# A two-layer cross-attention and mixture-of-experts kernel: the first experts' down product split into rounded parts, their up weights loaded tile by tile, and GpSimd's order and gathers changed

## The reference

```
x = x + attention0(layernorm(x), ctx)      # 16 heads
x = x + experts0(layernorm(x))             # top 1 of 8 by centroid; w1 (1024 x 256), relu, w2 (256 x 1024)
x = x + attention1(layernorm(x), ctx)      # 8 heads, two more layernorms, an output product
x = x + experts1(layernorm(x))             # top 2 of 8, gated by sigmoid, shared output product
```

## Time and profile before

| | us |
|---|---|
| median of 3 runs (1675.1 to 1678.51) | 1677.14 |
| the profiled execution | 1680.14 |
| its span, first to last instruction | 1678.3 |
| TensorE matmul busy (89% of the span) | 1491.0 |
| VectorE busy (60%) | 1002.0 |
| ScalarE busy (53%) | 882.1 |
| GpSimd busy (50%) | 833.9 |

### The profile page before, as it was taken

How to read it: one execution, slowest core, us unless ns; L and a number is a source line. 1 busy time by engine, 2 the same in 40 slices (tenths; PEclk the granted TensorE clock), 3 DMA queues, 4 the chain that set the end, 5 groups by cost and what they waited for, 6 DMA issues and landing times. The chain is left out here.

```text
span 1678.3 us, 50328 instructions
## 1 busy us (share of the span) xinstructions
PE 1491.0 (89%) x17142; PEld 1239.3 (74%) x17143; DVE 1002.0 (60%) x2228; ACT 882.1 (53%) x1626; POOL 833.9 (50%) x1145
## 2 busy tenths in 40 slices
PE   6999999999996499999599999999999646999677
PEld 4777777777774499999478888888888524888566
DVE  3677677677663433333247677777777577777544
ACT  3777777777774244443266566656665323333233
POOL 3576676666663111111256666666666305333263
PEclk8999999999996699999799999999999757999889
DMA  5111211110100611111212222221110042333475
GB/s 145 58 53 58 83 59 48 59 34 23 34 18 12 261 35 38 38 34 34 86 33 75 67 92 71 75 90 44 44 48 25 16 141 88 129 130 131 127 232 182
DMA packets 63184, 127.98 MB, mean 76 GB/s; under 512 B 11106, under 2 KB 35870, under 8 KB 59590
## 3 DMA queue, kind: packets, MB, share of 16 engines
q1 hardware_dynamic: 52798, 99.03, 18.2%
q0 software_dynamic: 10320, 28.07, 6.0%
HBM read 94.77 MB, written 32.29 MB: 76 GB/s over the span
## 5 line engine op out<-in xcount | busy, mean ns | idle before, releaser
L1017 DVE TENSOR_REDUCE a_mx<-a_SM 100x2 bf16<-100x722 f32 x384 | 351.4, 915 | 201.1 <-PE a_SM L459 197.8
L737 ACT ACTIVATE a_Pr<-a_ST 120x1600 f32<-120x1600 f32 (+3 forms) x192 | 225.0, 1172 | 125.5 <-PE a_ST L491 123.8
L501 PE MATMUL a_M<-a_Pr,a_V 120*32 120x100 f32 (+3 forms) x4608 | 176.2, 257 | 0.0
L459 PE MATMUL a_SM<-a_KT,a_QM 32*100 32x362 f32 x768 | 152.6, 393 | 25.9 <-DVE a_mx L1017 25.6
L787 POOL TENSOR_TENSOR a_rstd<-a_ve,a_powers 100x1 f32<-100x1 f32 x192 | 118.7, 618 | 96.2 <-DVE a_ve L986 94.5
L501 PEld LDWEIGHTS a_M<-a_Pr,a_V 120*32 120x32 f32 (+3 forms) x4608 | 135.8, 120 | 21.7 <-issue 12.8
L862 POOL TENSOR_TENSOR a_cl<-a_ct,a_ch 128x724 fp32r<-128x724 f32 x62 | 107.3, 1731 | 42.9 <-DVE a_o L1059 42.9
L386 PE MATMUL a_M<-a_wvh,a_ch 128*120 128x256 f32 (+1 forms) x384 | 123.8, 322 | 3.1 <-ACT a_KF L623 3.1
L852 POOL TENSOR_TENSOR a_KL<-a_KF,a_KT 128x724 fp32r<-128x724 f32 x64 | 111.5, 1742 | 26.7 <-ACT a_KT L631 15.4
L1534 PEld LDWEIGHTS e_PH<-e_xT,e_wS 128*128 128x128 f32 x1024 | 120.9, 194 | 4.2 <-issue 2.7
L1534 PE MATMUL e_PH<-e_xT,e_wS 128*128 128x128 f32 x1024 | 121.4, 277 | 2.1 <-DVE e_xT L1612 2.1
(11 more groups left out here) (219 smaller groups left out, 3872.3 us busy)
## 6 DMA issues: line engine op xcount, KB each, us to landing
w<-in_E_w SPq DMA_DIRECT2D x24, 1024.0 KB, 7.1
a_ct<-in_ctx SPq DMA_DIRECT2D x64, 362.0 KB, 3.2
gated_rows<-g_hs SPq DMA_DIRECT2D x57, 256.0 KB
keep_rows<-a_keep SPq DMA_DIRECT2D x64, 100.0 KB
tile_rows<-e_y SPq DMA_DIRECT2D x32, 128.0 KB, 1.7
X<-in_E_b SPq DMA_DIRECT2D x1, 4096.0 KB
x_rows<-X SPq DMA_DIRECT2D x32, 100.0 KB
g_xr<-x_rows SPq DMA_DIRECT2D x25, 128.0 KB
```

The lines of the kernel that those rows point to most:

```text
L459: last = nc.tensor.matmul(SM[0:LQ, half, 0:LKP], QM[b.p][rows, chunk, m, :], KT[b.p][rows, chunk, :], start=True, stop=True)
L501: last = nc.tensor.matmul(M0[VW * j:VW * (j + 1), g * LQ:(g + 1) * LQ], V[b.p][0:n, kt, h, :], Pr[0:n, kt, POS[h] * LQ:(POS[h] + 1) * LQ], ...
L737: nc.scalar.activation(Pr[0:n, s, :].rearrange("p (r q) -> p r q", r=GROUPS), ST[0:n, :, 0:PER * LQ], ACT.Exp, scale=SCALE).then_inc(exp_d ...
L1017: V_.tensor_reduce(pair, SM[0:LQ, :, 0:LK], AX_X, ALU.max).then_inc(max_done, 1)
```

## The change

It has four parts.

1. *Down product of the first experts.* Instead of 8 FP32 products there are 24 FP32R ones, from split operands. ScalarE makes `hT_high` from all of `hT` (`hidden_high`, 128 x 1024) once both halves of `hidden` are there. VectorE subtracts the low part of its half and GpSimd of the other (`hidden_low`, 128 x 512 each), in place: `hT_low[p]` lies on `hT[p]`. The expert's down weights are split for each tile: ScalarE makes `w2_high[p]` (`down_high`, 128 x 2048), VectorE `w2_low[p]` (`down_low`, 128 x 2048). TensorE's down waits for both halves of `hidden_low` and for `down_low`. VectorE's order in the loop becomes columns (j+2), hidden (j+1), hidden_low (j+1), down_low (j+1), finish (j).
2. *Up weights by transfer.* The buffer that the attention fills now holds the down weights. ScalarE's copy to `wS[p]` goes; SP loads the tile's expert's up weights, 1 MB, from device memory into `wS[p]` for each tile (`up_weights`), as soon as the up product two tiles earlier is done, ahead of the store of an earlier tile on its queue. Routing 0 loads no weights any more.
3. *GpSimd's order in the attentions' front.* The memsets of `V` move behind `cl`, `power` and `neg_ident`. TensorE waits for `pads_set` at 2; ScalarE waits for the finished `V` (`v_padded`) only before its first copies of values into it.
4. *Gathers with index columns in place.* In both experts the index copy and its wait go, the loops are written out, and the indirect transfer takes its column of `toks` directly. In the first experts `xs` becomes double, and gathers run two tiles ahead.

```diff
                     act.wait_ge(av_ps, b.count(1, -1))
+                if b.low <= 1:
+                    act.wait_ge(v_padded, 2)
                 act.wait_ge(v_ps, b.count(2, 1))
...
             nc.gpsimd.memset(powers[:, 1:2], -1.0)
             nc.gpsimd.memset(ones_bf[:], 1.0).then_inc(pads_set, 1)
-            nc.gpsimd.memset(V[0][:], 0.0).then_inc(pads_set, 1)
             pool.wait_ge(ch_ready, 1)
             nc.gpsimd.tensor_tensor(cl[0][:, 1], ct[0][:, 1], ch[0][:, 1], ALU.subtract).then_inc(cl_ready, 1)
             pool.wait_ge(pads_set, 1)
             power(0, fixed(0))
-            nc.gpsimd.memset(V[1][:], 0.0).then_inc(pads_set, 1)
             pool.wait_ge(loaded, FIRST_LOADED)
-            pool.wait_ge(pads_set, 3)
-            for p in range(2):
-                nc.gpsimd.memset(V[p][:, :, :, HD:HD + 1], 1.0)
             if layer == 0:
                 nc.gpsimd.tensor_copy(mask_bf[:], mask[:])
             nc.gpsimd.tensor_scalar(neg_ident[:], ident[0:LQ, 0:LQ], -1.0 / HD, 0.0, ALU.mult, ALU.add
                                     ).then_inc(pads_set, 1)
+            for p in range(2):
+                nc.gpsimd.memset(V[p][:], 0.0).then_inc(pads_set, 1)
             pool.wait_ge(pads_set, 4)
+            for p in range(2):
+                nc.gpsimd.memset(V[p][:, :, :, HD:HD + 1], 1.0).then_inc(v_padded, 1)
...
         xT = sb("xT", [128, DC, 128])
-        hT = [sb(f"hT{p}", [128, G, 128]) for p in range(2)]
+        hT_at = [(nc.sbuf_base + 31) // 32 * 32]
+        hT = [sb("hT0", [128, G, 128])]
+        hT_at.append((nc.sbuf_base + 31) // 32 * 32)
+        hT.append(sb("hT1", [128, G, 128]))
+        hT_low = [nc.alloc_sbuf_tensor_at(f"{tag}hT_low{p}", [128, G, 128], F32R, offset=hT_at[p]) for p in range(2)]
+        hT_high = [sb(f"hT_high{p}", [128, G, 128], F32R) for p in range(2)]
...
-            def store(j, p, r):
+            def up_weights(j, p, first):
+                e = expert_of(sp, j)
+                if not first:
+                    sp.wait_ge(h_ps, j * 2 - 2)
+                sp.dma_start(wS[p][:].rearrange("p c f -> p (c f)"),
+                             t["w1"][:, bass.ds(e, 1)].rearrange("p o c f -> p (o c f)")).then_inc(w_staged[p], 16)
+
+            def store(j, p):
                 sp.wait_ge(y_ready, j + 1)
                 sp.dma_start(t["ys"][bass.ds(j * 128, 128), :], y[p][:]).then_inc(y_stored[p], 16)
 
-            with sp.Fori(0, NT // 2) as i:
+            up_weights(0, 0, True)
+            up_weights(1, 1, True)
+            up_weights(2, 0, False)
+            with sp.Fori(0, NT // 2 - 2) as i:
                 for p in range(2):
-                    store(i * 2 + p, p, i)
-            if NT % 2:
-                store(NT - 1, 0, NT // 2)
-            sp.wait_ge(y_stored[0], 16 * ((NT + 1) // 2))
-            sp.wait_ge(y_stored[1], 16 * (NT // 2))
+                    up_weights(i * 2 + (p + 3), 1 - p, False)
+                    store(i * 2 + p, p)
+            for j in range(NT // 2 * 2 - 4, NT):
+                if j + 3 < NT:
+                    up_weights(j + 3, (j + 3) % 2, False)
+                store(j, j % 2)
+            for p in range(2):
+                sp.wait_ge(y_stored[p], 16 * (NT // 2))
...
-            def gather(j, first):
-
-                if not first:
-                    pool.wait_ge(x_ps, j)
-                pool.sem_inc(turns, 1)
-                nc.gpsimd.tensor_copy(gidx[:], env["toks"][:, bass.ds(j, 1)]).then_inc(idx_ready, 1)
-                pool.wait_ge(idx_ready, j + 1)
-                pool.sem_inc(turns, 1)
-                nc.gpsimd.indirect_dma_start(xs[:], None, t["keep"], bass.IndirectOffsetOnAxis(gidx[:], 0)
-                                             ).then_inc(rows_loaded, 16)
-
-            gather(0, True)
-            with pool.Fori(1, NT) as j:
-                gather(j, False)
-
-        def expert_of(engine, j):
-            return engine.value_load(env["tile_e"][0:1, bass.ds(j, 1)], min_val=0, max_val=E - 1)
+            def gather(j):
+                if j >= 2:
+                    pool.wait_ge(x_ps, j - 1)
+                nc.gpsimd.indirect_dma_start(xs[j % 2][:], None, t["keep"],
+                                             bass.IndirectOffsetOnAxis(env["toks"][:, j:j + 1], 0)
+                                             ).then_inc(rows_loaded[j % 2], 16)
+
+            def hidden_low(j):
+
+                p = j % 2
+                pool.wait_ge(h_high, j + 1)
+                nc.gpsimd.tensor_tensor(hT_low[p][:, 0:HALF].rearrange("p g q -> p (g q)"),
+                                        hT[p][:, 0:HALF].rearrange("p g q -> p (g q)"),
+                                        hT_high[p][:, 0:HALF].rearrange("p g q -> p (g q)"), ALU.subtract
+                                        ).then_inc(h_low_pool, 1)
+
+            gather(0)
+            gather(1)
+            for j in range(NT):
+                if j + 2 < NT:
+                    gather(j + 2)
+                hidden_low(j)
...
             def down(j, p, far):
-                e = expert_of(pe, j)
-                pe.wait_ge(hT_act, j + 1)
-                pe.wait_ge(hT_dve, j + 1)
+
+                pe.wait_ge(h_low_dve, j + 1)
+                pe.wait_ge(h_low_pool, j + 1)
+                pe.wait_ge(w2_low_ready, j + 1)
                 if far >= 2:
                     pe.wait_ge(y_ready, j - 1)
-                for g in range(G):
-                    rhs = w2[:, bass.ds(e, 1), g, :].rearrange("p o f -> p (o f)")
-                    last = nc.tensor.matmul(PY[:, p, 0:D], hT[p][:, g, :], rhs, start=(g == 0), stop=(g == G - 1))
+                steps = [(g, h, w) for g in range(G) for h, w in ((hT_high, w2_high), (hT_high, w2_low), (hT_low, w2_high))]
+                for k, (g, h, w) in enumerate(steps):
+                    last = nc.tensor.matmul(PY[:, p, 0:D], h[p][:, g, :], w[p][:, g, :],
+                                            start=(k == 0), stop=(k == len(steps) - 1))
                 last.then_inc(y_ps, 1)
...
-            def stage(j, p, first):
+            def hidden_high(j, p):
+                act.wait_ge(hT_act, j + 1)
+                act.wait_ge(hT_dve, j + 1)
+                nc.scalar.activation(hT_high[p][:].rearrange("p g q -> p (g q)"),
+                                     hT[p][:].rearrange("p g q -> p (g q)"), ACT.Copy).then_inc(h_high, 1)
+
+            def down_high(j, p, far):
                 e = expert_of(act, j)
-                if not first:
-                    act.wait_ge(h_ps, j * 2 - 2)
-                nc.scalar.activation(wS[p][:], w1[:, bass.ds(e, 1)].rearrange("p o c f -> p (o c) f"), ACT.Copy
-                                     ).then_inc(w_staged, 1)
-
-            stage(0, 0, True)
-            stage(1, 1, True)
+                if far >= 2:
+                    act.wait_ge(y_ps, j - 1)
+                nc.scalar.activation(w2_high[p][:].rearrange("p g d -> p (g d)"),
+                                     w2[:, bass.ds(e, 1)].rearrange("p o f -> p (o f)"), ACT.Copy
+                                     ).then_inc(w2_high_ready, 1)
+
+            down_high(0, 0, 0)
+            down_high(1, 1, 1)
             act.wait_ge(small_loaded, SMALL)
             for j in range(2):
                 hidden(j, j, j)
-                stage(j + 2, j, False)
+                hidden_high(j, j)
+            down_high(2, 0, 2)
             with act.Fori(1, NT // 2 - 1) as i:
                 for p in range(2):
                     hidden(i * 2 + p, p, 2)
-                    stage(i * 2 + (p + 2), p, False)
+                    hidden_high(i * 2 + p, p)
+                    down_high(i * 2 + (p + 1), 1 - p, 2)
             for j in range(NT - 2, NT):
                 hidden(j, j % 2, 2)
+                hidden_high(j, j % 2)
+                if j + 1 < NT:
+                    down_high(j + 1, (j + 1) % 2, 2)
...
+            def hidden_low(j, p):
+                dve.wait_ge(h_high, j + 1)
+                V_.tensor_tensor(hT_low[p][:, HALF:G].rearrange("p g q -> p (g q)"),
+                                 hT[p][:, HALF:G].rearrange("p g q -> p (g q)"),
+                                 hT_high[p][:, HALF:G].rearrange("p g q -> p (g q)"), ALU.subtract
+                                 ).then_inc(h_low_dve, 1)
+
+            def down_low(j, p):
+
+                e = expert_of(dve, j)
+                dve.wait_ge(w2_high_ready, j + 1)
+                V_.tensor_tensor(w2_low[p][:].rearrange("p g d -> p (g d)"),
+                                 w2[:, bass.ds(e, 1)].rearrange("p o f -> p (o f)"),
+                                 w2_high[p][:].rearrange("p g d -> p (g d)"), ALU.subtract).then_inc(w2_low_ready, 1)
...
             with dve.Fori(1, (NT - 2) // 2) as i:
                 for p in range(2):
-                    j = i * 2 + p
-                    hidden(j, p, 2)
-                    columns(j + 2, False)
-                    finish(j, p, i, 2)
-            for j in range(NT - 2, NT):
```

(80 more changed lines are left out.)

52 lines of the change are left out of this document (26 added, 26 removed).

## The result

The changed kernel takes 1684.49 us (median, 1683.48 to 1685.98) where the kernel before took 1677.14 beside it (1673.96 to 1680.52): a ratio of 1.0044, 95% interval 1.0028 to 1.0059, so 4.7 to 9.9 us slower. Forecast were 1710 and a range of 1682 to 1723. The direction was right; of the +33 us only +7 came.

What follows compares the result with a forecast made beforehand. TensorE was taken to bound the first experts at 7.25 us a tile, VectorE's chain afterwards at 8.70; +38.6 there, -3.9 attention fronts and -2 gathers made +32.7 on 1677.1, so 1710 us, range 1682 to 1723.

Steps and rivals of the forecast that it cites:

- issue before hidden: First experts, VectorE: idle time before hidden, behind the now longer columns, taken as 0.3 us a tile.
- issue before columns: First experts, VectorE: the 0.72 us gap seen behind finish, expected before columns, which now follow finish.
- exclusion: First experts: VectorE's two-input subtractions and GpSimd's half shut each other out; with it 8.7 us a tile, without 7.7.
- rival 2: First experts: TensorE stays the bound at 6.9 us a tile, exclusion and 1.3 us issue gone; 1661 us, chance 0.07.
- TensorE's side: First experts: 24 down products at 0.12 us, 2.9 for 3.45 us; tile of 6.7, with restart 6.9 us.
- Rival 1: First experts: no exclusion, halves side by side or GpSimd's behind down_low; 7.72 us a tile, 1682 us, chance 0.17.
- Rival 3: First experts: TensorE's idling lowers its clock too, adding 14 to 28 us; 1724 to 1738 us, chance 0.08.
- 28 tiles: First experts, columns of tile 3 to tile 31: 28 periods of 8.70 instead of 7.25 us, +40.6 us.
- start of the first experts: Before the first experts' steady part: earlier gathers against the wait for the first up weights, -2 us.
- tail: End of the first experts: VectorE's chain and one down product follow the last up product; 0, bounds -1 and +3 us.
- attention 1's front: Attention 1: TensorE's 2.88 us idle until GpSimd's neg_ident goes, since V's memsets move behind it; -2.9 us.
- first gather of the second experts: Second experts' start: first gather issues before VectorE's first w_low, without its copy; -2 us, between nothing and 3.

Runs made afterwards that it cites:

- shared_load: Changed kernel, but VectorE reads the expert's number for hidden and down_low once, ahead of columns, instead of once for each: 1675.67 us, ratio 0.9981 to the kernel before.
- pool_half_after: Changed kernel, but GpSimd's half of hidden_low waits until VectorE's down_low is done: 1691.04 us, ratio 1.0081 to the kernel before.
- whole_on_vector: Changed kernel, but VectorE subtracts all 1024 columns of hidden_low and GpSimd none: 1673.85 us, ratio 0.9975 to the kernel before.
- down_low_first_whole: Changed kernel with down_low ahead of hidden_low on VectorE, and hidden_low whole on VectorE: 1660.38 us, ratio 0.9893 to the kernel before.
- front_only: Kernel before the change with only part 3 (GpSimd's order in the attentions' front): 1675.62 us, ratio 0.9985 to the kernel before.
- first_whole_gather_done: down_low_first_whole, with VectorE's first w_low waiting for a one-column GpSimd memset behind the second experts' first gather: 1659.08 us, ratio 0.9890 to the kernel before.
- no_split: Changed kernel without part 1: down product in 8 FP32 products from unsplit operands, VectorE's order as before: 1674.06 us, ratio 0.9977 to the kernel before.

## Why the prediction was wrong

**The step that failed** is the sum of VectorE's period, "This sums to ... = 7.72 us a tile" and "A tile is then 7.72 - 0.3 + 1.28 = 8.70 us". By its terms:

| term, us | forecast | measured |
|---|---|---|
| columns, hidden, hidden_low, finish | 2.96 | 2.93 |
| hidden_high, as VectorE's wait | 1.16 | 1.19 |
| down_low, bare | 2.28 | 2.28 |
| GpSimd's half in its way | 1.28 | 0.94 |
| issue before hidden | 0.30 | 0.47 in every second tile, 0.23 on the mean |
| issue after hidden_low | 0 (0.3, put behind GpSimd's half) | 0.06 |
| issue before columns | 0.72 | none |
| overlap of the other neighbours, what is left | 0 | -0.17 |
| tile | 8.70 | 7.46 |

The bare durations were right to 0.03 us each. 0.72 of the 1.24 us is one term, taken as a constant; another 0.34 is the exclusion's size (below). The gap that VectorE showed before hidden in the earlier trace rows, behind finish, was carried over to columns, which now follows finish. That gap is register work of the sequencer (0.305 + 0.19 + 0.02 us and a few short steps for each number read), which goes on while earlier instructions run. It shows only as far as it lasts longer than they do. Before, it began with finish, which ran for only 0.42 us. Now the numbers of finish and columns are read under 3.2 us of down_low (the reads start at 699.55 and 700.78, while down_low runs from 699.52 to 702.74). The number for hidden is read only from 703.26, just after columns has begun (703.00), and that leaves the 0.47; in the other tile, without the loop's jump, its read starts at 710.35, ahead of columns (710.73), and nothing is left. The four reads, each from a window of its own of the view by source line:

```profile
L1491 DVEq TENSOR_LOAD <-tile_e x1: 306/306/306, 699.5 to 699.5; - x1
...
L1491 DVEq TENSOR_LOAD <-tile_e x1: 305/305/305, 700.8 to 700.8; - x1
...
L1491 DVEq TENSOR_LOAD <-tile_e x1: 307/307/307, 703.3 to 703.3; - x1
...
L1491 DVEq TENSOR_LOAD <-tile_e x1: 305/305/305, 710.4 to 710.4; - x1
```

shared_load shows it from the other side: moved under down_low, the remaining 0.47 goes too. The forecast had named this itself, under rival 2 ("registers may be worked out while VectorE waits"), and priced it at 1.3 us; that rival was given a chance of 0.07.

The Trainium skill (Perfetto Trace Analysis, "Sequencer Loop") says that a sequencer pushes engine instructions into a queue and reads on, and that the instruction waits there for its semaphores. The reads under down_low agree with it. But it doesn't read on without end. While hidden_low waited for ScalarE, nothing behind it was read: down_low's own number was read only from 706.51, when hidden_low was released (706.50).

**The exclusion** was right in kind. The Trainium skill's rule (SBUF — State Buffer, "Who interferes with whom") holds with these forms: 3.22 beside GpSimd's half, 2.28 without it. Its size was not: the forecast laid the three bare durations end to end, and they overlap as printed. From the end of hidden_low to that of GpSimd's half it is 1.14 us (707.19 to 708.33), from there to the end of down_low 2.14 (to 710.47). The bare durations are 1.27 (pool_half_after) and 2.28 (whole_on_vector). So, by these numbers, each began 0.13 to 0.14 us before the printed end of the one ahead of it. Without the half, down_low would have ended 0.06 + 2.28 = 2.34 us after hidden_low and not 3.28, and 0.94 is the price. In shared_load down_low is printed as 3.37, grown by 1.09, but only because its printed start lies 0.08 us before the end of hidden_low and not 0.06 behind it; the two stretches are 1.15 and 2.14 again (702.24, 703.39, 705.53).

**TensorE's side** was right to 0.04: 24 products at 0.12 us, a dense tile of 6.66 (forecast 6.7, with a restart 6.9). Rival 2, TensorE the faster bound, is what down_low_first_whole makes true: 28 x (6.66 - 7.25) = -16.5 us.

**Rival 1** (no exclusion, 1682) is the nearest in time and has the wrong mechanism: the exclusion is there. That 1684 lies inside the stated range at all is luck, since only this rival stretched the range so far down. Its second form, GpSimd's half behind down_low "where only TensorE waits for it and has 2 us to spare", was run as pool_half_after: TensorE has nothing to spare, since its rows feed VectorE's columns. **Rival 3**, the clock: 1.00 in the steady part of this stage, so it did not happen.

**The other steps**, on the profiled span, with what each missed:

| step | forecast | measured | difference |
|---|---|---|---|
| 28 tiles | +40.6 | +5.9 | -34.7 |
| start of the first experts | -2 | -1.0 | +1.0 |
| tail | 0 | +1.1 | +1.1 |
| attention 1's front | -2.9 | -2.3 | +0.6 |
| attention 0 and routing 0 | -1 | +0.7 | +1.7 |
| attention 1 behind its front, routing 1 | 0 | +2.4 | +2.4 |
| first gather of the second experts | -2 | +0.2 | +2.2 |
| rest of the second experts | 0 | -2.0 | -2.0 |
| sum | +32.7 | +5.0 | -27.7 |

*Start*: the row numbers to the columns of tile 3, 29.31 us before, 28.34 after. *Tail*: columns of tile 31 to the memset of `powers`, 26.21 and 27.32. *Rest of the second experts*: front_only, whose second experts are those of the kernel before, is 2.4 us faster there too, so the -2.0 says nothing of the change. *Attention 1's front*: neg_ident is early now, and the product of the earlier trace rows waits 1.51 us for ScalarE's `xh` in place of 2.88 for neg_ident:

```profile
832.76 0.56 PE L422 MATMUL a_M<-a_ident,a_xh 100*128 100x100 f32 x2 [1.51 <-ACT a_xh L655]
```

`xh` needs GpSimd's power, which the edit moved forward only by one memset; the bound had been the idle time, and something else stood just behind it.
*First gather*: "before VectorE's first w_low" didn't come true. Timeline of the changed kernel, as the earlier trace rows:

```profile
1395.97 4.48 DVE L1999 TENSOR_TENSOR w_low<-w,w_high 128x2048 fp32r<-128x2048 f32 x2
...
1396.44 2.75 POOL L1839 DMA_INDIRECT g_xs<-keep_rows,toks  x1 [43.18 <-POOLq L107]
...
1402.51 0.66 PE L1866 MATMUL g_PX<-kept_ident,g_xs 128*128 128x128 f32 x2 [9.29 <-DMA g_xs<-keep_rows,toks]
```

w_low starts 0.47 us ahead and shuts GpSimd out. In first_whole_gather_done even a free gather brought only 0.5.

**What stays open.** Attention 1, from its 5th to its 125th maximum, at the full clock, takes 456.2 us before and 458.2 after. The instructions are the same. front_only (456.1) and no_split (456.7) are near to the first, shared_load (457.2), whose attention 1 is that of the changed kernel, lies between, and the other split versions (457.8 to 458.5) to the second. The cause is open: there is one profile of each kernel, so how much this stage varies from run to run isn't known, and the place of the instructions in memory would be only a guess. These 2 us are a part of the 7.4.

## What to carry to other kernels

An "issue" gap in a profile belongs to its neighbours: ask what the sequencer does in it, from which release on, and what runs ahead of it in the new order, before it goes into a sum as a constant. When a wait between two engines stands in the middle of the busiest queue, look for an instruction of that queue that needs neither side of it: one swap of down_low and hidden_low turned +0.4% into -0.8%. And two-input VectorE subtractions share badly with GpSimd. Here, giving GpSimd half of one saved 0.54 us and cost 0.94; VectorE alone was better in both orders.

## What was not expected of the hardware

- A gather's issue on GpSimd takes 0.95 us where no two-input subtraction of VectorE stands in its way (whole_on_vector), and 2.84 at the median in the changed kernel. There 28 of the 32 end 0.83 or 0.84 us after down_low: they are shut out until it is nearly done, and then take their bare time. A GpSimd instruction shut out by VectorE is printed with the wait inside its duration, with no idle time before it.
- The exclusion is passed on in turns: with down_low (2.29, not lengthened) running, GpSimd's half takes 2.24 for 1.27, and VectorE's next instruction 1.76 for 0.69. As in the changed kernel, each begins, by the bare durations, 0.13 to 0.15 us before the printed end of the one ahead.
- A semaphore raised by GpSimd's sequencer behind a gather came 0.2 us before the gather had started; one raised by the end of a memset behind the gather came 0.1 us after the gather's issue had ended.
